# A one-core linear-attention kernel with a quantised layer behind it: another order of its stages, and other banks

## The reference

```python
h = layernorm(x)
q, k, v = phi(h @ Wq.T + bq), phi(h @ Wk.T + bk), h @ Wv.T + bv      # phi = elu + 1, 16 heads of 32
kv_cum, k_cum = cumsum(k (x) v, over tokens), cumsum(k, over tokens)
att = (q . kv_cum) / max(q . k_cum, 1e-6)
x = x + layernorm(att @ Wo.T + bo)                                   # "o", its residual is "r"
r = mx_quantise(layernorm(x))                                        # blocks of 32, scaled, rounded, scaled back
x = x + layernorm(r @ mx_quantise(weight).T + bias)                  # "f"
```

## Time and profile before

| | |
|---|---|
| time, median of 3 runs | 2627.73 us (2625.16 to 2629.82) |
| the profiled execution | 2631.21 us, of it the span 2629.4 us |
| TensorE busy | 2518.0 us, 96% of the span |
| VectorE busy | 2148.7 us, 82% |
| ScalarE busy | 1143.0 us, 43% |
| GpSimd busy | 1055.4 us, 40% |
| mean granted TensorE clock | 0.992 |

### The profile page before, as it was taken

How to read it: one execution, slowest core, us unless ns; L and a number is a source line. 1 busy time by engine, 2 the same in 40 slices (tenths; PEclk the granted TensorE clock), 3 DMA queues, 4 the chain that set the end, 5 groups by cost and what they waited for, 6 DMA issues and landing times.

```text
span 2629.4 us, 62366 instructions
## 1 busy us (share of the span) xinstructions
PE 2518.0 (96%) x24082; PEld 2062.7 (78%) x24082; DVE 2148.7 (82%) x4177; ACT 1143.0 (43%) x2058; POOL 1055.4 (40%) x1482
## 2 busy tenths in 40 slices
PE   5999999999999999999999999999999999999996
PEld 4778778778778778778787787787787877877885
DVE  6788888888888888888888888888888888888885
ACT  4444444444444444444444444444444444444442
POOL 1234444344443334443334433344433444434443
PEclk8999999999999999999999999999999999999998
DMA  4011101111011111011111011110111110011110
GB/s 151 20 43 48 42 30 32 40 48 44 30 38 40 40 48 44 28 34 38 48 48 35 30 39 40 48 44 28 40 38 42 48 41 31 32 40 48 32 33 17
DMA packets 57483, 107.55 MB, mean 41 GB/s; under 512 B 6768, under 2 KB 7152, under 8 KB 56816
## 3 DMA queue, kind: packets, MB, share of 16 engines
q1 hardware_dynamic: 57456, 107.18, 12.7%
HBM read 73.60 MB, written 33.55 MB: 41 GB/s over the span
## 4 chain that ended last, share of the span: by engine, by line
PE 45%; DVE 37%; issue 11%; ACT 4%; POOL 2%; DVEq 1%; ACTq 0%; POOLq 0%; DMA 0%; SPq 0%
PE work L343 10%; PE work L345 8%; PE work L344 8%; DVE kc L830 6%; PE score L434 4%; PE work L360 4%; PE work L460 4%; DVE QT L811 3%; PE work L453 3%; DVE A L873 3%; DVE KT L811 3%; DVE bn_x L788 2%; DVE amax L898 2%; DVE bn_r L788 2%; DVE bn_f L788 2%
## 5 line engine op out<-in xcount | busy, mean ns | idle before, releaser
L873 DVE TENSOR_TENSOR A<-score,causal 128x512 f32<-128x512 f32 x512 | 317.5, 683 | 42.7 <-PE score L434 42.7
L597 ACT ACTIVATE o_buf<-x_res,shift_r,rs_r 128x512 f32<-128x512 f32 x128 | 104.3, 815 | 395.6 <-POOL shift_r L1048 395.6
L1055 POOL TENSOR_TENSOR x_res<-x_res,o_buf 128x512 f32<-128x512 f32 x128 | 179.4, 1402 | 209.5 <-ACT o_buf L597 209.5
L593 ACT CAST xT_hi<-work 128x512 fp32r<-128x512 f32 x128 | 74.6, 583 | 396.5 <-PE work L360 396.5
L343 PE MATMUL work<-wv_hi,xT_hi 128*128 128x512 f32 x512 | 216.9, 424 | 0.0
L343 PE MATMUL score<-xT_hi,wk_hi 128*128 128x512 f32 x512 | 208.4, 407 | 6.3 <-issue 6.3
L343 PE MATMUL work<-wo_hi,oT_hi 128*128 128x512 f32 x512 | 206.2, 403 | 2.9 <-DVE oT_lo L880 2.6
L1045 POOL TENSOR_TENSOR rs_f<-ve_f,minus_half 128x1 f32<-128x1 f32 x128 | 70.1, 548 | 342.6 <-DVE ve_f L792 342.6
L343 PE MATMUL score<-xT_hi,wq_hi 128*128 128x512 f32 x512 | 205.1, 401 | 0.0
L345 PE MATMUL work<-wo_hi,oT_lo 128*128 128x512 f32 x512 | 203.3, 397 | 0.0
L344 PE MATMUL work<-wo_lo,oT_hi 128*128 128x512 f32 x512 | 203.1, 397 | 0.0
(11 more groups left out here) (130 smaller groups left out, 6750.6 us busy)
## 6 DMA issues: line engine op xcount, KB each, us to landing
x_in<-in_x SPq DMA_DIRECT2D x128, 256.0 KB, 2.9
x_res<-in_x SPq DMA_DIRECT2D x128, 256.0 KB, 2.6
out<-f_buf SPq DMA_DIRECT2D x96, 256.0 KB, 2.0
out<-xd SPq DMA_DIRECT2D x32, 256.0 KB, 2.0
V<-in_wk SPq DMA_DIRECT2D x1, 1024.0 KB, 7.1
QT<-in_wq SPq DMA_DIRECT2D x1, 1024.0 KB, 7.9
kc<-in_wo SPq DMA_DIRECT2D x1, 1024.0 KB, 9.7
A<-in_wf SPq DMA_DIRECT2D x1, 1024.0 KB, 11.5
```

The costliest lines, as they stand in the source:

```text
L873: nc.vector.tensor_tensor(A[:, j, :, :], score_bank[j][:], causal[:].unsqueeze(1).to_broadcast([P, G, P]), ALU.mult).then_inc(a_set, 1)
L1055: nc.gpsimd.tensor_tensor(x_res[:, b, :], x_res[:, b, :], o_buf[:, b % 2, :], ALU.add).then_inc(r_set, 1)
```

## The change

TensorE: v(0) moves in front of den; f(3) moves in front of spread; v(1), v(2) and v(3) each come one place earlier: v(1) stands between spread and sc(0), v(2) between sc(0) and x(0), v(3) ahead of o(0), and o(1) alone between sc(2) and x(2). The banks of fifteen stages are others; attend(3) has W2, which kn(3) had. VectorE: quantise(1) moves behind phi_k(0), o_bias(3) behind xd_lo(0), r_stats(2) and r_stats(3) and quantise(2) and quantise(3) later, scan(1) behind f_stats(0), quantise(0) behind mask(3) and x_lo(3), o_bias(2) and r_stats(1) behind o_lo(3), f_bias(3) in front of the divides; o_bias(2) and o_bias(3) now also wait for q8_set of the sequence that had their half of o_buf. ScalarE: the norms of o and r behind k(0), k(1), k(2), xd_hi(1); f_norm(1) in front of q(2); f_norm(3) behind f_norm(2). GpSimd: rstd(o,3) in front of rstd(r,2), dequantise(3) in front of product(0). Two bias tiles of 16 bytes a partition are placed last, and a spacer of 256 bytes a partition stands in front of xdT_hi1. No arithmetic is added or taken away.

```diff
@@ -35,11 +35,11 @@
...
     (("o", 3), W0), (("xd", 0), W1), (("f", 0), W2), (("xd", 1), W1), (("f", 1), W0), (("xd", 2), W1),
-    (("f", 2), W2), (("xd", 3), W1), (("den", 0), W0), (("v", 0), W2), (("kn", 0), W1), (("f", 3), W0),
-    (("v", 1), W1), (("x", 0), W2), (("att", 0), W0), (("kn", 1), W2),
-    (("v", 2), W1), (("o", 0), W2), (("x", 1), W0), (("att", 1), W1), (("kn", 2), W0),
-    (("v", 3), W2), (("o", 1), W0), (("x", 2), W1), (("att", 2), W2), (("kn", 3), W1),
-    (("x", 3), W0), (("o", 2), W1), (("att", 3), W0),
+    (("f", 2), W2), (("xd", 3), W1), (("v", 0), W0), (("den", 0), W2), (("kn", 0), W1), (("f", 3), W0),
+    (("v", 1), W1), (("v", 2), W2), (("x", 0), W0), (("att", 0), W1), (("kn", 1), W2),
+    (("v", 3), W0), (("o", 0), W1), (("x", 1), W2), (("att", 1), W0), (("kn", 2), W1),
+    (("o", 1), W2), (("x", 2), W0), (("att", 2), W1), (("kn", 3), W2),
+    (("x", 3), W0), (("o", 2), W1), (("att", 3), W2),
 ]
@@ -75,8 +75,6 @@
...
         bias_k = sb("bias_k", [P, G])
-        bias_q_plus_1 = sb("bias_q_plus_1", [P, G])
-        bias_k_plus_1 = sb("bias_k_plus_1", [P, G])
         minus_bias_q = sb("minus_bias_q", [P, G])
@@ -120,6 +118,8 @@
...
         xd = sb("xd", [P, D])
+
+        sb("spacer", [P, 64])
         xdT_hi1 = sb("xdT_hi1", [P, G, P], F32R)
@@ -135,6 +135,8 @@
...
         w_amax = sb("w_amax", [P, G * NBLK])
+        bias_q_plus_1 = sb("bias_q_plus_1", [P, G])
+        bias_k_plus_1 = sb("bias_k_plus_1", [P, G])
 
@@ -393,6 +395,8 @@
...
                         take(i, ("v", b), here, before)
+                        if first and b == 0:
+                            pe.wait_ge(wf_lo_set, G)
                         weights(i, "v")
@@ -400,7 +404,6 @@
...
                         if first:
-                            pe.wait_ge(wf_lo_set, G)
                             pe.wait_ge(small_loaded, 16 * N_SMALL)
@@ -524,19 +527,20 @@
...
                 xd_transposes(3)
+                v(0)
                 denominators()
-                v(0)
                 kn(0)
+                f(3)
                 spread()
-                f(3)
+                v(1)
                 scores(0)
-                v(1)
+                v(2)
                 x_transposes(0)
...
                 scores(1)
-                v(2)
+                v(3)
                 if cur:
@@ -544,7 +548,6 @@
...
                 scores(2)
-                v(3)
                 if cur:
@@ -668,25 +671,27 @@
...
 
-                if prev:
-                    o_norm(i - 1, 2)
                 k(0)
...
                     high("q")
+                if prev:
+                    r_norm(i - 1, 1)
+                    o_norm(i - 1, 2)
                 xd_hi(0)
-                if prev:
-                    r_norm(i - 1, 2)
-                    o_norm(i - 1, 3)
                 k(1)
...
                     high("o")
+                if prev:
+                    o_norm(i - 1, 3)
                 k(2)
                 if prev:
-                    r_norm(i - 1, 3)
+                    r_norm(i - 1, 2)
                 k(3)
...
                 xd_hi(1)
+                if prev:
+                    r_norm(i - 1, 3)
                 f_norm(0)
@@ -694,8 +699,8 @@
...
                     wf_high(1)
+                f_norm(1)
                 q(2)
-                f_norm(1)
                 q(3)
@@ -706,23 +711,21 @@
...
                 f_norm(2)
+                f_norm(3)
                 if nxt:
...
                 kn(1)
-                f_norm(3)
                 if nxt:
...
                 state(1)
+                kn(2)
                 if cur:
                     o_norm(i, 0)
-                kn(2)
-                if cur:
-                    r_norm(i, 0)
                 if nxt:
@@ -730,11 +733,11 @@
...
                 if cur:
-                    o_norm(i, 1)
+                    r_norm(i, 0)
                 if nxt:
...
                 if cur:
-                    r_norm(i, 1)
+                    o_norm(i, 1)
                 o_hi(3)
@@ -882,6 +885,8 @@
...
                     dve.wait_ge(o_mm, count(tile, b))
+                    if b >= 2:
+                        dve.wait_ge(q8_set, count(tile, b - 2))
                     nc.vector.tensor_tensor(o_buf[:, b % 2, :], bank(("o", b))[:], bias_o[:],
@@ -926,34 +931,35 @@
...
 
-                if prev:
-                    quantise(i - 1, 1)
-                    r_stats(i - 1, 2)
                 phi_k(0)
...
                 if prev:
+                    quantise(i - 1, 1)
+                xd_lo(0)
+                if prev:
                     o_bias(i - 1, 3)
-                xd_lo(0)
-                if prev:
-                    quantise(i - 1, 2)
                 phi_k(1)
...
                     low("o")
+                if prev:
+                    r_stats(i - 1, 2)
                 scan(0)
-                if prev:
-                    r_stats(i - 1, 3)
                 phi_k(2)
...
                     quantise_wf()
-                scan(1)
+                if prev:
+                    r_stats(i - 1, 3)
                 f_bias(0)
                 f_stats(0)
-                if prev:
-                    quantise(i - 1, 3)
+                scan(1)
+                if prev:
+                    quantise(i - 1, 2)
                 phi_k(3)
...
                 scan(2)
+                if prev:
+                    quantise(i - 1, 3)
                 phi_q(0)
@@ -980,22 +986,23 @@
...
                 xd_lo(3)
+                v_bias(0)
                 invert()
                 f_stats(2)
-                v_bias(0)
+                f_bias(3)
                 for b in range(NSEQ):
                     divide(b)
+                f_stats(3)
+                v_bias(1)
                 if nxt:
                     x_stats(i + 1, 3)
-                f_bias(3)
                 mask(0)
-                v_bias(1)
-                f_stats(3)
+                v_bias(2)
                 if nxt:
...
                 mask(1)
-                v_bias(2)
+                v_bias(3)
                 if cur:
@@ -1004,21 +1011,19 @@
...
                     r_stats(i, 0)
-                v_bias(3)
-                if cur:
                     o_bias(i, 1)
...
                 o_lo(2)
+                mask(3)
+                if nxt:
+                    x_lo(i + 1, 3)
                 if cur:
                     quantise(i, 0)
-                mask(3)
-                if nxt:
-                    x_lo(i + 1, 3)
+                o_lo(3)
                 if cur:
+                    o_bias(i, 2)
                     r_stats(i, 1)
-                    o_bias(i, 2)
-                o_lo(3)
 
@@ -1080,20 +1085,21 @@
...
                     residual(i - 1, 2)
-                    rstd(i - 1, "r", 2)
                     dequantise(i - 1, 1)
                     rstd(i - 1, "o", 3)
+                    rstd(i - 1, "r", 2)
                     residual(i - 1, 3)
...
                 output(0)
+                if prev:
+                    dequantise(i - 1, 3)
                 product(0)
...
                 if prev:
-                    dequantise(i - 1, 3)
                     rstd(i - 1, "f", 1)
@@ -1103,10 +1109,10 @@
...
                 output(2)
+                if prev:
+                    rstd(i - 1, "f", 3)
                 if nxt:
                     rstd(i + 1, "x", 3)
-                if prev:
-                    rstd(i - 1, "f", 3)
                 output(3)
@@ -1115,8 +1121,8 @@
...
                     dequantise(i, 0)
+                    rstd(i, "o", 2)
                     rstd(i, "r", 1)
-                    rstd(i, "o", 2)
 
```

More of the change, by code:

```diff
@@ L935, in turn @@
                 if prev:
-                    o_bias(i - 1, 3)
+                    quantise(i - 1, 1)
                 xd_lo(0)
                 if prev:
-                    quantise(i - 1, 2)
+                    o_bias(i - 1, 3)
                 phi_k(1)
@@ L1012, in turn @@
                 o_lo(2)
-                if cur:
-                    quantise(i, 0)
                 mask(3)
@@ L1018, in turn @@
                 if cur:
+                    quantise(i, 0)
+                o_lo(3)
+                if cur:
+                    o_bias(i, 2)
                     r_stats(i, 1)
-                    o_bias(i, 2)
-                o_lo(3)
             for b in range(NSEQ):
```

## The result

The changed kernel takes 2714.15 us, median of 4 runs (2713.51 to 2715.15), against 2628.78 us for the kernel before on the same chip (4 runs, 2625.16 to 2629.89). The ratio is 1.0327 (95% interval 1.0312 to 1.0343): slower by 85 us. The profiled execution has a span of 2711.9 us and a mean granted clock of 0.978, where before had 2629.4 and 0.992.

A forecast was written before the change was run, and what follows sets the result against it. TensorE bounds the kernel, VectorE nearly full. New waits of 1.0 + 3.3 + 1.1 = 5.4 us against 2.4 removed: +3.0 in 31 turns, plus 1, 94 us; forecast 2722 us, own range 2700 to 2745, wider range 2607 to 2765.

The forecast's parts named there:

- Waits removed, and where VectorE takes them back: TensorE: 2.4 us a turn removed at den and attend(3); new waits of 1.0 at f(1), 3.3 at f(2).
- The walk through VectorE's order: VectorE from mask(3) to xd_lo(2): operations placed one by one, 7.3 us idle and lost where the old order had 4.2.
- the 31 us of that step: VectorE/GpSimd: rstd's power waits for scan(0), delaying residual(3) and r_stats(3); if it did not, the sum is 31 us smaller.
- Den's new wait: TensorE at den: waits 1.1 us a turn for f_bias(2), late because f_norm(1) goes ahead of q(2).
- rival 3: TensorE's clock falls behind f(2)'s wait each turn, f(2) takes 5.2 instead of 2.8: +40 us, 2762; chance 0.14.
- My reason against it: Against the clock falling at f(2): the drain's wait followed small matmuls, f(2)'s follows two full products.
- Nothing for the addresses: Bias columns and spacer move addresses only: zero effect, since matmuls take 0.233 us whatever the operands.
- 17 either way: Bound on the address effect: 1% of the 240 would be 0.56 us a turn, 17 in all.
- 77.6: TensorE's turn without waits: 80.04 less 2.4 us, number of matmuls unchanged.
- Prologue: Before the steady turns: the wait for wf_lo moves ahead of v(0), once, within 1 us.
- the forecast's range: Whole kernel as walked: 2700 to 2745 us, chance 0.45.

The follow-up runs named there:

- g4_front: Changed kernel with VectorE, ScalarE and GpSimd orders between mask(3) and f(2) essentially as before; TensorE order, banks, placement and VectorE's den-to-mask(2) order kept: 2557.93 us, ratio 0.9735.
- g1_fnorm: Changed kernel with ScalarE's f_norm(1) back behind q(2): 2688.89 us, ratio 1.0232 to the kernel before.
- g2_output: Changed kernel with GpSimd's output(0) moved behind product(1), away from scan(2): 2735.91 us, ratio 1.0407 to the kernel before.
- g3_tail: Changed kernel with quantise(0) back ahead of mask(3), o_bias(2) ahead of o_lo(3), r_norm(0) ahead of state(2): 2708.87 us, ratio 1.0304 to before.
- g7_scan1: Changed kernel with VectorE's scan(1) back ahead of r_stats(3), f_bias(0) and f_stats(0): 2719.17 us, ratio 1.0336 to the kernel before.
- n_noplace: Changed kernel without the placement, bias tiles back and no spacer: 2723.9 us, ratio 1.0355 to the kernel before.
- g8_xstats: g5_xdlo with x_stats(0) ahead of scan(3) on VectorE: 2537.47 us, ratio 0.9646 to the kernel before.
- p_both: Kernel before with only the change's placement, two bias tiles last and the spacer in front of xdT_hi1: 2615.49 us, ratio 0.9942.
- g5_xdlo: g4_front with xd_lo(1) ahead of phi_k(3) on VectorE: 2553.71 us, ratio 0.9712 to the kernel before.
- p_bias: Kernel before with only the two 16-byte bias tiles moved to the end: 2617.26 us, ratio 0.995.
- p_pad: Kernel before with two unused tiles of the same size added behind the bias tiles: 2627.93 us, ratio 0.9996.

## Why the prediction came out right, step by step

- **Waits removed, and where VectorE takes them back.** Right. Den and attend(3) wait no longer on kc and xT_lo. f(1) waits 1.02 us (I said 1.0), f(2) 3.08 (3.3): means over 28 turns of the start-to-start times less 2.72. `g4_front` shows the cause apart: the old order of the k and q part takes f(2)'s wait away altogether. That undoes several places at once, so which share each of them has was not measured except for those that `g1_fnorm`, `g2_output`, `g3_tail` and `g7_scan1` touch.
- **The walk through VectorE's order.** Its idle times and collisions came where it put them: 0.88, 0.68, 0.56 and 1.10 us idle (said 1.0, 0.7, 0.7, 1.2), the multiply 0.58 longer (0.65), the copy behind scan(2) 0.91 longer (1.05), scan(3) 0.50 (0.6) and its copy 0.91 (0.8). Only the copies behind scan(0) and scan(1), priced at 0.3 each, lost nothing (0.17). The power of rstd behind a scan, for which the rows of before had no case, takes 1.42 instead of 0.55, and r_stats(3) waited for x_res, as the 31 us of that step required. This agrees with the rule of the Trainium skill, "SBUF — State Buffer", section "Who interferes with whom", that VectorE with two SBUF inputs and GpSimd reading SBUF lock each other out. Xd_lo(1) ended 0.3 and xd_lo(2) 0.6 us earlier than walked.
- **Den's new wait: mis-sized by the clock.** Said 1.1 in each turn. It is 1.19 in the 8 of 28 steady turns in which f(2) takes 2.83 us, and nothing in the other 20, since f(2) ends 1.4 to 2.4 us later there: 0.34 on average. Its cause is f_norm(1) ahead of q(2), as said: `g1_fnorm` removes it.
- **The clock: rival 3 came in part, and cost a quarter of its price.** The clock fell behind f(2)'s wait in 20 of 28 turns; in 16 f(2) takes 4.2 to 4.4 us, in 4 it takes 5.26. But those 16 turns last 82.7 to 82.9 us, against 82.47 for the turns at full clock, and the 4 last 84.05: den's wait swallows most. That is about 16 x 0.3 + 4 x 1.6 = 11 us, where the rival had 40: it took the whole of f(2) for slow in each turn, and only 4 of 28 are so. My reason against it, that two full products stand ahead of the wait, did not hold.
- **Nothing for the addresses: mis-sized.** The products became up to 0.07 us faster, 9.8 us for this order (`n_noplace`), within the 17 either way that I had given as the bound. The reading behind the zero was at fault: the two equal means of 0.233 us a matmul were made of unequal parts, f at 2.79 to 2.80 us a product, k(2) at 2.75 and those behind transposes at 2.84, so they could not show that the rate has nothing to do with the operands. Without any wait a turn is 77.0 us, not 77.6: 82.88 less 1.02, 3.08, 1.2 (f(2) at its clock), 0.34 and 0.2 (the first matmuls behind a wait). `g8_xstats`, at 77.10 with almost no wait, agrees. `n_noplace` less its own waits (0.79, 3.05, 1.06, 0.36, 0.07) is 77.7, and its 2723.9 us lies 2 from the forecast.
- **Prologue: mis-sized.** I priced it within 1 us. From the first k(0) to the second it is 4.1 us shorter. The placement has a part in it (85.3 us in `p_both` against 87.3 before) and so has the order (84.3 in `n_noplace`); which edit of the order was not tested.

So 82.88 us a turn against 83.0 is in part a cancelling: 0.6 less for the faster products, 0.8 less at den and 0.2 less at f(2), against 1.2 for the clock and 0.2 behind the waits. Den and the clock belong together, since the slow f(2) covers den's wait: the turns at full clock last 82.47 us, 0.5 under the forecast, and the clock puts 0.4 back. The sign, the places and the size of f(1)'s and f(2)'s waits were right and would have given some 2702 us at full clock, still in the forecast's range; that a turn came within 0.1 us was luck.

## What to carry to other kernels

Moving work off the busiest engine's path pays only if the next engine's order still meets the new dates: here one half of the reordering was worth 71 us and the other, made with it, cost 156; run the two apart. Walk the second engine's order through the new schedule with start-to-start times, and write at each operation with two SBUF operands, and at the small copies, what GpSimd is doing at that moment: an idle time filled with such an operation can become a collision of the same length (`g7_scan1`), and statistics with a single SBUF operand put in the place of a scan take the collision away (`g8_xstats`). A wait that you shorten is worth only what the next chain leaves of it (`g2_output`, `g5_xdlo`).

## What the runs showed of the hardware

- Two tiles of 16 bytes a partition, moved behind all other tiles, make matmuls of 512 columns up to 2.6% faster (0.233 to 0.227 us each, `p_bias`); a shift the other way makes some 0.02 us a product faster and some up to 0.05 slower (`p_pad`). No row shows why.
- A wait of 3.1 us a turn is followed by the lower clock in 20 of 28 turns; one of 2.5 us (`g2_output`) in 14 of 31, and in 15 of the other 17 den's of 2.1 is; those of 0.4 and 0.7 (`g5_xdlo`, `g4_front`) never are, nor f(1)'s of 1.0. Behind the same wait at f(2) the low clock comes in 29 and 30 of 31 turns in `g3_tail` and `g7_scan1`, but in 17 of 31 in `g1_fnorm`. It is no accident which turns: in the kernel after they last 82.47, 82.47, 82.87, 82.86, 84.05, 82.89, 82.67 us and then the same again, in `g3_tail` they repeat by fours, in `g7_scan1` and `n_noplace` by threes. What sets the pattern stays open. A wait that costs the clock anew agrees in kind with the loop in the Trainium skill's "TensorE: Matmul & The Clock Gate", section "HAM oscillation — how this bites in real kernels", but here the clock falls in some turns and not in others behind the same wait.
- A 128x1 power on GpSimd and a 128x4 copy on VectorE, small as they are, wait for the end of the other engine's operation (1.42 us instead of 0.55, 1.08 instead of 0.17).
